# Attention chunks of eight slots instead of four, weighted rows and old sums in PSUM, one reduction per chunk (a graph kernel on one core)

## What is computed

```python
xw = (x @ W).reshape(n_nodes, H, C)
al_s = jnp.einsum('nhc,hc->nh', xw, a_src)
al_d = jnp.einsum('nhc,hc->nh', xw, a_dst)
logits = jax.nn.leaky_relu(al_s[src] + al_d[dst], LRELU_SLOPE)
m = jax.lax.stop_gradient(jax.ops.segment_max(logits, dst, num_segments=n_nodes))
e = jnp.exp(logits - m[dst])
denom = jax.ops.segment_sum(e, dst, num_segments=n_nodes)
alpha = e / denom[dst]
out = jax.ops.segment_sum(alpha[:, :, None] * xw[src], dst, num_segments=n_nodes)
```

## Time and profile before

| | us |
|---|---|
| runs: median of 3 | 5300.02 |
| runs: lowest and highest | 5288.86, 5310.14 |
| profiled execution | 5343.62 |
| its span | 5342.1 |
| mean granted TensorE clock, share of full speed | 0.574 |

### The profile page before, as it was taken

One profiled execution on the slowest core, in us unless ns is written; L12 is line 12 of the kernel. 1 busy time (PEld: TensorE's weight loads), 2 busy tenths in 40 slices (PEclk: granted clock), 3 DMA queues, 4 the chain that ended last, 5 costly groups with the idle time before them and its releaser, 6 DMA issues. The chain is left out here.

```text
span 5342.1 us, 42226 instructions
## 1 busy us (share of the span) xinstructions
PE 810.9 (15%) x8458; PEld 603.3 (11%) x8458; DVE 3110.0 (58%) x8318; ACT 593.4 (11%) x1962; POOL 2869.6 (54%) x2942
## 2 busy tenths in 40 slices
PE   1666774230000000004200000000030000000002
PEld 0555553110000000003100000000030000000001
DVE  5888522346666766674566766666624544444453
ACT  2222310120000000002100000000030000000001
POOL 2000011356766666662666666666546666666663
PEclk9777787665555555557655555555575555555555
DMA  2222565124333333332433333333313222222222
GB/s 63 100 94 108 207 209 203 46 69 92 95 93 95 92 93 94 94 92 42 89 92 93 95 91 94 94 95 94 74 33 46 49 47 47 49 49 47 49 48 21
DMA packets 183101, 451.07 MB, mean 84 GB/s; under 512 B 99948, under 2 KB 101810, under 8 KB 178205
## 3 DMA queue, kind: packets, MB, share of 16 engines
q0 software_dynamic: 122928, 318.15, 25.5%
q1 hardware_dynamic: 15246, 126.96, 6.3%
q10 hardware_dynamic: 44784, 4.00, 0.7%
HBM read 392.10 MB, written 57.22 MB: 84 GB/s over the span
## 5 line engine op out<-in xcount | busy, mean ns | idle before, releaser
L482 POOL DMA_INDIRECT rows_all<-gat_tab,ell_list x2664 | 2606.9, 979 | 1279.9 <-issue 870.8
L1564 DVE TENSOR_TENSOR rows_all<-rows_all 128x528 f32<-128x528 f32 (+3 forms) x1332 | 672.8, 505 | 426.4 <-remote 256.3
L1558 DVE TENSOR_TENSOR rows_all<-rows_all,banks 128x1024 f32<-128x1024 f32 (+1 forms) x666 | 690.0, 1036 | 0.0
L1005 PE MATMUL banks<-ident,x_st 128*128 128x128 f32 x260 | 56.6, 303 | 3911.0 <-PEq L121 3911.0
L789 ACT ACTIVATE banks<-ex_in 128x40 f32<-128x40 f32 x666 | 138.3, 208 | 3610.7 <-ACTq L121 2835.6
L1005 PEld LDWEIGHTS banks<-ident,x_st 128*128 128x128 f32 x260 | 43.7, 211 | 3915.4 <-issue 3915.2
L1545 DVE COPY lrel<-acc 128x8 f32 x666 | 123.7, 186 | 493.4 <-DVE acc L1567 197.0
L1567 DVE TENSOR_TENSOR acc<-acc,rows_all 128x264 f32 (+1 forms) x666 | 260.4, 391 | 112.0 <-DVE rows_all L1564 77.7
L1556 DVE TENSOR_TENSOR acc<-acc,banks 128x264 f32 (+1 forms) x666 | 254.3, 382 | 0.4
L482 POOL DMA_INDIRECT edges<-sw_d,edge_pick x28 | 32.3, 1154 | 413.1 <-POOLq L121 401.0
L1547 DVE SCALAR_TENSOR_TENSOR lrel<-score 128x32 f32<-128x32 f32 x666 | 128.8, 193 | 211.0 <-DVE score L1546 106.5
(11 more groups left out here) (269 smaller groups left out, 1898.8 us busy)
## 6 DMA issues: line engine op xcount, KB each, us to landing
rows_all<-gat_tab,ell_list POOLq DMA_INDIRECT x2664
x_t<-adj_d SPq DMA_DIRECT2D x11, 3328.0 KB
y_t<-adj_d SPq DMA_DIRECT2D x11, 3328.0 KB
adj_d<-x_t SPq DMA_DIRECT2D x7, 3328.0 KB, 10.0
adj_d<-y_t SPq DMA_DIRECT2D x6, 3328.0 KB, 10.4
ell_list<-ell_d ACTq DMA_DIRECT2D x224, 7.5 KB
acc<-key_d SPq DMA_DIRECT2D x1, 1664.0 KB, 6.4
acc<-vec_d SPq DMA_DIRECT2D x1, 1664.0 KB
```

The lines of the kernel that those rows point to most:

```text
L482: return g.indirect_dma_start(out=dst, out_offset=None, in_=table, in_offset=bass.IndirectOffsetOnAxis(ap=idx, axis=0))
L1558: made = link.mark(v.tensor_tensor(msg, msg, exp_ps[u][:, 0:SLOTS, :].unsqueeze(3).to_broadcast([P, SLOTS, HEADS, c]), ALU.mult))
L1564: link(v.tensor_tensor(low, low, high, ALU.add))
```

## The change

A chunk has eight slots, and the ring three buffers (24 slots as before). A list holds one chunk, so there are three list buffers, and GpSimd waits for a chunk's list ahead of its gathers. LAG is 1: two tokens at the start, so that the gathers of chunk k may start once chunk k-2 has its exponentials. `tile_known` is gone, and VectorE loads the tile's number inside `weigh`.

PSUM banks 0 to 4 hold nine slots of a row's width (`msg_ps`), one set for all chunks. ScalarE writes all nine exponentials, once, into the score column of the nine slots. VectorE writes the old sums times their exponential into the ninth slot and the rows times theirs into the other eight, and one `tensor_reduce` over the nine slots writes the new sums to SBUF. It replaces the adds. `weigh` and `fold` of one chunk follow each other, without the next chunk's `weigh` in between. Unchanged lines of `weigh` are cut.

```diff
-SLOTS = 4
+SLOTS = 8
...
-RING = 6
+RING = 3
...
-LISTED = 3
+LISTED = 1
...
-LAG = 2
-AHEAD = 2
+LAG = 1
...
+        exp_warm = sb("exp_warm", [P, HEADS])
...
-        exp_ps = [banks[:, (0, 1, 7)[u % 3], u // 3 * 64:u // 3 * 64 + (SLOTS + 1) * HEADS].rearrange("p (r h) -> p r h", h=HEADS) for u in range(RING)]
-        shrink = [exp_ps[u][:, SLOTS, :] for u in range(RING)]
+        msg_ps = banks[:, 0:5, :].rearrange("p b n -> p (b n)")
...
-        tile_known = sem("tile_known")
...
-            def known_list(n):
-                take(pool, ell_landed[n], 16)
-                pool.sem_inc(tile_known, 1)
-
             def chunk_gathers(layer, table, width):
                 with pool.Fori(0, rounds) as it:
                     for u in range(RING):
+                        if u % LISTED == 0:
+                            take(pool, ell_landed[u // LISTED], 16)
                         take(pool, rows_free)
                         for r in range(SLOTS):
                             gather(rows[u][:, r * width:(r + 1) * width], table, ell[u][:, r:r + 1])\
                                 .then_inc(rows_landed[u], 16)
-                        if u % LISTED == LISTED - 1:
-                            known_list((u + 1) // LISTED % LISTS)
...
-            known_list(0)
...
-                s.activation(shrink[RING - 1], zero_t[:, 0:HEADS], ACT.Exp)
+                msg_h = msg_ps[:, 0:(SLOTS + 1) * width].rearrange("p (r h q) -> p r h q", h=HEADS, q=c + 1)
+                act_chain(s.activation(exp_warm[:, :], zero_t[:, 0:HEADS], ACT.Exp))
                 act.wait_ge(ell_wrapped, 16)
                 with act.Fori(0, rounds) as it:
                     for u in range(RING):
                         take(act, exp_in)
-                        s.activation(exp_ps[u], ex_in[:, :, :], ACT.Exp).then_inc(rows_free, 1)
-                        s.activation(rows[u][:, 0:SLOTS * width].rearrange("p (r h q) -> p r h q", h=HEADS, q=c + 1)[:, :, :, c],
-                                     ex_in[:, 0:SLOTS, :], ACT.Exp).then_inc(exp_done, 1)
+                        s.activation(msg_h[:, :, :, c], ex_in[:, :, :], ACT.Exp).then_inc(exp_done, 1)
+                        act.sem_inc(rows_free, 1)
                         if u % LISTED == LISTED - 1:
                             load_list(u // LISTED, (it + 1) * RING)
...
-            tile_reg = [dve.alloc_register(f"tile_of_chunk{n}") for n in range(AHEAD + 1)]
-
-            def load_tile(u):
-
-                if u % LISTED == 0:
-                    take(dve, tile_known)
-                dve.reg_load(tile_reg[u % (AHEAD + 1)], ell[u][0:1, TILE_AT:TILE_AT + 1])
-
             def chunk_tile(u):
-                return dve.snap(tile_reg[u % (AHEAD + 1)], min_val=0, max_val=T - 1)
+                return nc.values_load(ell[u][0:1, TILE_AT:TILE_AT + 1], engines=(mybir.EngineType.DVE,), min_val=0, max_val=T - 1,
+                                      skip_runtime_bounds_check_because="list_tile writes the numbers of T tiles and no others")
...
-                def weigh(u, tile, turn):
-
-                    dve.wait_ge(rows_landed[u], (turn + rounds * l + 1) * GROUP)
-                    signal(ticks["dve"])
...
-                    v.tensor_tensor(ex_in[:, :, :], lrel[:, :, :], m_all[:, now, :].to_broadcast([P, SLOTS + 1, HEADS]), ALU.subtract)\
-                        .then_inc(exp_in, 1)
-
-                def fold(u, tile):
-
-                    at = sums_h[:, bass.ds(tile, 1), :, :].rearrange("p a h q -> p (a h) q")
-                    dve.wait_ge(exp_done, u + 1)
-                    v.tensor_tensor(at, at, shrink[u].unsqueeze(2).to_broadcast([P, HEADS, c + 1]), ALU.mult)
-                    msg = row_h[u][:, :, :, 0:c]
-                    made = link.mark(v.tensor_tensor(msg, msg, exp_ps[u][:, 0:SLOTS, :].unsqueeze(3).to_broadcast([P, SLOTS, HEADS, c]), ALU.mult))
-                    load_tile((u + AHEAD) % RING)
-                    link.wait(made)
-                    half = SLOTS // 2
-                    while half:
-                        low, high = rows[u][:, 0:half * width], rows[u][:, half * width:2 * half * width]
-                        link(v.tensor_tensor(low, low, high, ALU.add))
-                        half //= 2
-                    at = tile_of(sums, tile)
-                    link(v.tensor_tensor(at, at, rows[u][:, 0:width], ALU.add))
-
-                def one_round(turn, last):
-
-                    now = chunk_tile(0)
+                msg_h = msg_ps[:, 0:(SLOTS + 1) * width].rearrange("p (r h q) -> p r h q", h=HEADS, q=c + 1)
+                by_slot = msg_ps[:, 0:(SLOTS + 1) * width].rearrange("p (r w) -> p w r", w=width)
+
+                with dve.Fori(0, rounds) as it:
+
+                    def weigh(u):
+
+                        dve.wait_ge(rows_landed[u], (it + rounds * l + 1) * GROUP)
+                        signal(ticks["dve"])
+                        tile = chunk_tile(u)
+                        now = bass.ds(tile, 1)
...
+                        v.tensor_tensor(ex_in[:, :, :], lrel[:, :, :], m_all[:, now, :].to_broadcast([P, SLOTS + 1, HEADS]), ALU.subtract)\
+                            .then_inc(exp_in, 1)
+                        return tile
+
+                    def fold(u, tile):
+
+                        at = sums_h[:, bass.ds(tile, 1), :, :].rearrange("p a h q -> p (a h) q")
+                        dve.wait_ge(exp_done, u + 1)
+                        link.mark(v.tensor_tensor(msg_h[:, SLOTS, :, :], at, msg_h[:, SLOTS, :, c].unsqueeze(2).to_broadcast([P, HEADS, c + 1]), ALU.mult))
+                        made = link.mark(v.tensor_tensor(msg_h[:, 0:SLOTS, :, 0:c], row_h[u][:, :, :, 0:c],
+                                                         msg_h[:, 0:SLOTS, :, c].unsqueeze(3).to_broadcast([P, SLOTS, HEADS, c]), ALU.mult))
+                        link.wait(made)
+                        link(v.tensor_reduce(tile_of(sums, tile), by_slot, AX.X, ALU.add))
+
                     for u in range(RING):
-                        if u + 1 < RING or not last:
-                            after = chunk_tile((u + 1) % RING)
-                            dve.wait_ge(exp_done, u + 1)
-                            weigh((u + 1) % RING, after, turn + (u + 1) // RING)
-                        fold(u, now)
-                        now = after
+                        fold(u, weigh(u))
                     link.reset()
                     signal(exp_done, -RING)
-
-                if l == 0:
-                    for u in range(AHEAD):
-                        load_tile(u)
-                weigh(0, chunk_tile(0), 0)
-                link.reset()
-                with dve.Fori(0, rounds - 1) as it:
-                    one_round(it, False)
-                one_round(rounds - 1, True)
```

More of the change, by code:

```diff
@@ L820, in _ @@
                     last.then_inc(silu_done, high - low)
-            for n in range(1, LISTS):
+            for n in range(LISTS):
                 act.wait_ge(ell_landed[n], 16)
```

9 lines of the change are left out of this document (4 added, 5 removed).

## The result

| | before | after |
|---|---|---|
| median of 16 runs | 5299.71 us | 5324.51 us |
| their range | 5288.46 to 5316.80 us | 5317.94 to 5329.54 us |
| profiled execution | 5343.62 us | 5324.92 us |
| its span | 5342.1 us | 5323.3 us |
| ratio of times | | 1.0041, 95% interval 1.0032 to 1.0050 |

The change makes the kernel 0.4% slower: 25 us, inside what I had called no change. The forecast was 5510 us, 210 us more than before. Note that the profiled execution of before lies above all 16 of its other runs (5343.62 us against at most 5316.80), and that of after among its own.

The account below looks back on a forecast made before the run. Bound: a cost of every gather, hidden from engine busy times, at some 1.457 us. Profiled 5343.6 us plus 210 for added gathers, other terms zero, gave 5554, scaled to the median: 5510 us; range 5170 to 5680, likeliest case 5420 to 5580.

Parts of the forecast that it names:

- The bound: Attention loops: something every gather costs, shown by neither engine's busy time, sets some 1.457 us per gather in all layers.
- Number of gathers: Attention loops: 936 gathers instead of 888, 48 more per layer, all padding; 210 us in all, the only term on the path.
- VectorE's new prices: VectorE per chunk of eight, layers 0 and 1: reduction 2.66 us, rows' product 2.28 us, 7.7 us in all.
- rival 3: VectorE in layers 0 and 1 becomes the bound, reduction at 5.1 us: 82 us more each, 5670 us; chance 0.07.
- Covered by GpSimd: VectorE's saving and lost overlap lie beside GpSimd's eight gathers (10.3 us own pace, 11.7 measured): zero.
- At 1.457 us: 69.9 us per layer: Attention loops: the 48 added gathers per layer priced at the old kernel's pace, 210 us in all.
- Buffers: Ring, still 24 slots: GpSimd pauses 4 to 6 us as now, so about as much is lost per gather.
- rival 1: Attention loops: VectorE's slow spells fade and gathers shorten; together about -370 us, 4930 us, half of that 5115; chance 0.26.
- Rival 2: Attention loops: semaphore updates of every kind set the pace; 1.374 us per gather, -8 us per layer, 5275 us; chance 0.14.
- The sum's frame: Whole kernel: profiled 5343.6 us + 210 = 5554, lowered because the runs' median is 0.8% under it, to 5510 us.

Follow-up runs that it names:

- the deeper ring: Kernel before with nine row buffers instead of six (900 gathers per layer): 5404.49 beside 5306.54 us with pauses, 1.0194; without pauses 1.0127.
- the reduction alone: Kernel before, chunks of four and order of work kept, with only the PSUM product and single reduction: 5281.52 beside 5353.55 us with pauses, 0.9862.

## Why the prediction was wrong

*The bound, right as a description.* A pace per gather, equal in the three layers, that neither engine's busy time shows, is in the profile of after too (1.377, 1.377, 1.375 us), and the deeper ring (1.444, 1.445, 1.439) shows that it doesn't come from the number of buffers. But it isn't a price of the gather alone: eight updates on ScalarE, shorter lists and the reduction each move it (1.0125, 0.9953, 0.9862) at the same number of gathers.

*Number of gathers, right.* 2808, and without pauses the 144 more are what makes it slower: 126 us measured, 193 us less with 144 gathers left out. VectorE's new prices were right to about 1% (2632 against 2660 ns, 2289 against 2280), so rival 3 had nothing to stand on.

*Covered by GpSimd, right without pauses,* but with less to spare than I gave it: chunks of four in the new order are VectorE-bound (+107 us). With pauses it isn't shown: there VectorE's chunk of 11.2 us stands at GpSimd's pace, and no run with pauses has the lost overlap alone.

*The step that failed is "At 1.457 us: 69.9 us per layer".* I kept the pace of the kernel before for a kernel whose gathers and steps are others, and wrote under *Buffers* that "about as much is lost per gather". In the profiles the idle time above the gap fell from 0.162 to 0.126 us per gather in layer 0. By the medians the pace went from 1.440 to (5324.5 - 1465.2) / 2805 = 1.376 us. 144 gathers at 1.440 us are +207 us; 2805 intervals shorter by 0.065 us are -182 us; the sum is the +25 measured. Of these 0.065 us:
- 0.027 came with the adds' going: the reduction alone does it (0.9862), on the one chip where it ran. I had the shorter gather in rival 1, 41 us in each of two layers, and left it out of the sum because the pace seemed to belong to something else than GpSimd. That was the error in reasoning. Layer 2 has a shorter gather at the same pace, with longer pauses (175 us above the gap against 144): that says that the two trade against each other there, and not that no part of the change moves the pace. For the same reason it stays open whether the shorter gather is what pays.
- Up to 0.020 may come from VectorE's and ScalarE's semaphore updates: some 14 per chunk of eight instead of four, 1.75 fewer per gather, at the measured 12 ns. This is an extrapolation of ScalarE's added updates to the ones removed, so it is argued.
- The rest, 0.018 or more, stays open. That `weigh` and `fold` no longer interleave is a candidate that wasn't isolated with pauses.

*A rival that no run tests* covers all of it. By the code VectorE waits on its own semaphore seven times per chunk of four in the kernel before, five times in the reduction alone and five times per chunk of eight in the changed kernel: 0.50 and 1.13 fewer per gather. The pace fell by 0.027 and 0.065 us, which is 0.054 and 0.058 us for each wait that went. Adding such waits alone, with pauses, would test it. A set price per wait can't be the whole of it, as layer 2's longer waits at the same pace show. So the step that failed is known, the pace carried over, and what sets the pace with pauses stays open.

*Rival 2 gave the right number for the wrong reason.* Its pace of 1.374 us is close to the 1.376 measured (its 5275 us are 50 under the 5324.5), but it rested on every landing counting as an update does, and the lists (0.9953 for an expected 1.024) and the eight updates (12 ns each, not 65) speak against it. A forecast by it would have been lucky.

*Rival 1, in part.* The pauses faded from some 150 to 120 us per layer, not to nothing; as the profiled execution of before was 43 us above its median, some 15 us of that per layer may be the execution. In the other condition the rival's pace is fully there, 1.257 us per gather, but in the kernel before too (1.272).

*The sum's frame.* The profiled execution of before was 43 us above its median, so the pace of 1.457 read from it was 1.440 in the median run. I scaled the total by 0.8%; if the stretches outside the loops take the same 1467 us in both, the whole difference lies in the loops, and they should have been scaled. It matters little to the sum, 5300 + 207 = 5507 us.

## What to carry to other kernels

Where an engine's issue of gathers sets the pace, count the gathers, padding among them: doubling a chunk's slots to save VectorE work added 5% here, which ate the gain. The part of the change that pays (0.986 alone, with pauses; not run without) is the one that takes VectorE's two-input SBUF adds away from beside the gathers; take it without the larger chunks. A pace that is read off a trace and whose cause isn't known must not be carried over to a kernel that changes what runs beside it; read first whether its parts trade against each other.

## What the runs showed of the hardware that I had not expected

- One kernel has two times, 5300 and 4800 us, on the same chip, with VectorE's long instructions the same length (the product 1214 ns, the sums' product 426 ns in both). What differs is the time around semaphores, and GpSimd's pauses with it: without pauses each of VectorE's steps behind its own semaphore follows in some 0.035 us, with pauses many only after 0.5 us or more, and of ScalarE's added updates, 17 ns otherwise, a part takes 0.7 us. What makes one or the other is open.
- With pauses the trace of before holds 22,080 records of semaphore updates, and that of the nearly equal kernel without pauses 66,140; of after 13,025 and 65,767. All eight kept traces with pauses lack them so, and none of the twelve without: of landings alone they hold 7,000 to 13,800 records against 52,000 to 56,600. So the delivery of the updates or of their records may be backed up where the pauses are. This is a correlation; no run here takes it apart, or tells whether the recording itself has a part in it.
- In the layers with 264 elements a gather takes 969 to 1000 ns by the mean in the kernels with two-input adds in SBUF, single ones up to 1.48 us and, beside adds of 1056 elements and fewer in a row, 2.00 us; without these adds it takes 945 to 949 ns by the mean and never over 1.01 us.
- A reduction over a stride of 264 elements in PSUM costs 1.04 ns per element and some 160 ns (2632, 1532 and, with a stride of 136, 1432 ns for 2376, 1320 and 1224 elements), the same as the product (2289 and 1222 ns for 2048 and 1024).
